# The output projection of a selective scan's reversed parts: from one block of work at steps 48 to 52 to two halves at steps 35 and 48

## The chip, the cores and the metric

The kernel runs on one core of a Trainium2 chip. The metric is device time of the whole launch in microseconds (us). The program is one launch of a four-layer network; the change touches only its first layer.

## The reference, cut to what matters

Layer 0 is a bidirectional selective scan (Mamba) on 2 images of 48 x 48 = 2304 tokens, 256 channels, 512 inner channels, 16 states. Layers 1 to 3 (linear attention, softmax attention, a graph mixture, sigmoid attention, a mixture of experts) follow and are not touched.

```python
def step(h, xs):                       # d_inner = 512, n = 16 states
    d_t, B_t, C_t, u_t = xs
    dA = jnp.exp(d_t[..., None] * A)
    h = dA * h + (d_t * u_t)[..., None] * B_t[:, None, :]
    y = jnp.einsum('bdn,bn->bd', h, C_t)
    return (h, y)
# a branch: xs = silu(causal depthwise conv(xi)); proj = xs @ xproj_w.T
#           dt = softplus(proj[:16] @ dtproj_w.T + b); B, C = rest of proj
#           y = (scan + xs * D) * silu(z)
# layer: xi, z = in_proj(norm(x)); forward branch + branch over the reversed tokens;
#        out = x + out_proj(y_forward + y_reversed)
```

## The kernel before, in words

`mamba_chunks` cuts each image into 5 parts of 461 tokens (`MT`; the last 460). A part takes 64 steps (`STEPS`), one for each of 16 states x 4 blocks of 128 inner channels. The 20 parts are numbered g = 0 to 19: 0 to 4 forward over image 0, 5 to 9 reversed over image 0, 10 to 14 and 15 to 19 the same for image 1. h is the next part, g + 1. Steps are counted S = 64 g + s.

At each step ScalarE (ACT) writes the exponential `DA(S)` into a PSUM bank (L778), GpSimd (POOL) multiplies `DBU` (L919), VectorE (DVE) runs the scan over the tokens (L963) and multiplies by C (`mix`, L974), and TensorE (PE) adds the product to y in PSUM with an identity matrix (L607, two passes in float32). DVE works in pairs of steps: two scans, mix, a small copy of the carried states, mix. ACT runs ahead of DVE by at most two scans, since there are two banks for `DA`; POOL by four; DVE may be ahead of PE by four products (`G` has four buffers).

Everything else is laid between the steps, at fixed step numbers written out by hand in each engine's loop: an engine works its own list in order, so what it waits for holds up the step's instruction behind it. While part g is scanned, the engines prepare part h: convolution (PE s = 11, 13, 16, 19; ACT takes it at 16 to 28: `take_conv`, `exp_conv`, `log_conv`, `sig_conv`), `xproj` (PE 36, ACT `take_pj` 44), `dt(h, 0)` (PE 42, ACT `dt_part` 47 to 52, `floor_rest` 56, POOL's sums at 52 to 63), and `dt(g, 1)` at 5. The gate z of a reversed part h is projected on PE at 55, 56, 59, 61 (`z`, L550) and taken by ACT at 58 to 63 (`take_z` L730, `exp_z` L735). `xi` (L492) projects the input of forward part g + 2. `first` (L590, L592) opens the four y banks 0 to 3 with D * xs and the stored forward y; `gate_y` (L951, DVE) multiplies the finished y of a reversed part by silu(z): blocks 0 and 1 at s = 34 of the part, 2 and 3 at s = 2 of the next.

The output projection of a reversed part is done during the part behind it: `out(g - 1, m, half)` on PE at s = 48, 49, 51, 52, m being the block of 128 output channels. It adds x (loaded into `XR`) with the identity (L564, 2 passes) and 4 products with `w_out` (L566, 8 passes) into PSUM bank m. ACT copies both banks into X at once at s = 55 (`take_out`, L754). This is so in parts 6 to 10 and 16 to 19; the last, part 19, is projected after the loop.

PSUM banks 0 to 3 hold y of the running part. Blocks 0 and 1 are finished with step 31, and from `gate_y` (or, in a forward part, `take_y` at ACT's step 35) until the next part begins banks 0 and 1 are free for xproj (bank 0), dt (0 and 1), the output projection, z and xi (0 and 1 in turn). Semaphores with the names `dt_base`, `o_ready`, `o_added`, `z_exp`, `y_taken` guard these uses.

The lines before the change that matter most:

```python
if is_rev(g - 1):
    if s == 48:
        out(g - 1, 0, 0)
    elif s == 49:
        out(g - 1, 0, 1)
    elif s == 51:
        out(g - 1, 1, 0)
    elif s == 52:
        out(g - 1, 1, 1)
...
if s == 55 and is_rev(g - 1):
    take_out(g - 1)
```

Of the kernel before, what the change touches and what calls it, by code (L numbers as in the profile page):

```python
# [313 lines left out]
def mamba_chunks(nc, ctx, k, A, w):  # L314
# [62 lines left out]
    with nc.Block() as block:  # L377
        @block.sync
        def _(sp):
# [43 lines left out]
            for g in range(NCH):  # L423
# [7 lines left out]
                if is_rev(g - 1):  # L431
                    b, at, n = tokens(g - 1)
                    if rev_before(g - 1):
                        sp.wait_ge(o_added, rev_before(g - 1))
                    sp.dma_start(XR[:, :, :n], A["x"][b].rearrange("(k p) n -> p k n", p=P)[:, :, at:at + n])\
                      .then_inc(xr_in, 16)
# [37 lines left out]
            sp.wait_ge(o_added, rev_before(NCH - 1))  # L474
            sp.dma_start(XR[:, :, :n], A["x"][b].rearrange("(k p) n -> p k n", p=P)[:, :, at:at + n]).then_inc(xr_in, 16)
            sp.wait_ge(o_added, rev_before(NCH))

        @block.tensor
        def _(pe):
            def xi(h, j):  # L480
                b, at, n = tokens(h)
                if j < 2 and h:
                    pe.wait_ge(dt_base, 2 * (h - 1) + 1)
                    if h >= 2 and rev_before(h - 2):
                        pe.wait_ge(o_added, rev_before(h - 2))
                    if is_rev(h - 1):
                        pe.wait_ge(z_exp, JD * rev_before(h))
# [40 lines left out]
            def dt(h, p):  # L528
                rev = chunk(h)[1]
                pe.wait_ge(pj_done, h + 1)  # L530
                if p:
# [9 lines left out]
            def z(h, j):  # L541
                b, at, n = tokens(h)
                if j < 2:
                    pe.wait_ge(dt_base, 2 * h + 1)
                    if rev_before(h - 1):
                        pe.wait_ge(o_added, rev_before(h - 1))
# [7 lines left out]
            def out(g, m, half):  # L554
                if half == 0:
                    pe.wait_ge(y_taken, 2 * g + 2)
                    if g + 2 < NCH:
                        pe.wait_ge(dt_base, 2 * (g + 2) + 1)
                    elif g + 1 < NCH:
                        pe.wait_ge(y_taken, 2 * (g + 1) + 1)  # L560
                    if rev_before(g):
                        pe.wait_ge(o_added, rev_before(g))
                    pe.wait_ge(xr_in, 16 * (rev_before(g) + 1))
                    pe.matmul(PS[:, m, :wide(g)], k.ident[:], XR[:, m, :wide(g)], start=True, stop=False)  # L564
                for j in range(2 * half, 2 * half + 2):
                    mm = pe.matmul(PS[:, m, :wide(g)], w.w_out[:, j, m * P:(m + 1) * P], Z[:, g % 2, j, :wide(g)],  # L566
                                   start=False, stop=(j == JD - 1))
                if m == 1 and half == 1:
                    mm.then_inc(o_ready, 1)

            def first(g, p):
                rev = chunk(g)[1]
                pe.wait_ge(xs_done, JD * (g + 1))
                if p == 0:
                    pe.wait_ge(dt_base, 2 * g + 1)
                    if g and rev_before(g - 1):
                        pe.wait_ge(o_added, rev_before(g - 1))
# [25 lines left out]
            for S in range(STEPS * NCH):  # L603
# [7 lines left out]
                if h < NCH:  # L611
# [10 lines left out]
                    elif s == 42:  # L622
                        dt(h, 0)
                if is_rev(g - 1):
                    if s == 48:
                        out(g - 1, 0, 0)
                    elif s == 49:
                        out(g - 1, 0, 1)
                    elif s == 51:
                        out(g - 1, 1, 0)  # L630
                    elif s == 52:
# [3 lines left out]
                if is_rev(h):  # L635
                    if s == 55:
                        z(h, 0)
                    elif s == 56:
                        z(h, 1)
                    elif s == 59:  # L640
                        z(h, 2)
                    elif s == 61:
# [12 lines left out]
        def _(act):  # L655
# [68 lines left out]
            def take_z(h, j):  # L724
# [3 lines left out]
                if j == 0 and taken:  # L728
                    act.wait_ge(o_ready, taken)
# [21 lines left out]
            def take_out(g):  # L751
                b, at, n = tokens(g)
                act.wait_ge(o_ready, rev_before(g) + 1)
                act.activation(k.X[:, :, b * L + at:b * L + at + n], PS[:, 0:KC, :n], ACT.Copy).then_inc(o_added, 1)  # L754
# [16 lines left out]
            for S in range(STEPS * NCH):  # L771
# [13 lines left out]
                if h < NCH:  # L785
# [14 lines left out]
                    elif s == 24:  # L800
                        take_conv(h, 3)
                    elif s == 25:
                        exp_conv(h, 3)
                    elif s == 26:
                        sig_conv(h, 0)
                    elif s == 27:
                        log_conv(h, 1)
                    elif s == 28:
# [7 lines left out]
                if s == 55 and is_rev(g - 1):  # L816
                    take_out(g - 1)
                if s == 35 and is_fwd(g):
                    take_y(g, 0)
                if is_rev(h):  # L820
                    if s == 58:
                        take_z(h, 0)
                    elif s == 59:
                        exp_z(h, 0)
# [29 lines left out]
            take_out(NCH - 1)  # L854
# [2854 lines left out]
```

## Time and profile before

| | us |
|---|---|
| median of 3 runs | 5767.82 |
| the runs | 5745.86, 5767.82, 5774.27 |
| the profiled execution | 5744.21 |
| its span | 5742.4 |
| first scan step to last of layer 0 | 150.7 to 2343 |

The span is the time from the first to the last instruction; the profiled execution's own time is 1.8 us longer. TensorE's mean granted clock is 0.928 of full speed. Over the whole span PE is busy for 4796.9 us (84%), DVE 3422.7 (60%), ACT 2068.0 (36%), POOL 2320.9 (40%); these are averages over stages with different limits. In timelines a float32 matmul shows as two passes, and passes that follow one another overlap in the record.

### The profile page before, as it was taken

To read this page: it belongs to the slowest core of one execution; us is meant where nothing else is said; L and a number is where in the kernel's file an instruction comes from. 1 tells how busy PE (TensorE), PEld (TensorE's weight loads), DVE (VectorE), ACT (ScalarE), POOL (GpSimd) and SP (SyncE) were. 2 spreads that over 40 slices of the span, in tenths; PEclk is the share of its full clock that TensorE was granted. 3 is DMA by queue.
4 is the path that set the end of the run, shared out by engine and by line. 5 is a ranking of instruction groups with operands and counts; after the bars stand their busy time and mean duration, and the time that the engine had idled before them with its cause. 6 is when DMAs were issued, how large, how long until landed. Compare 5 with 4: busy or idle time off the path is not lost. (4 is left out here: it accounts for less than half of the span.)

```text
span 5742.4 us, 53254 instructions
## 1 busy us (share of the span) xinstructions
PE 4796.9 (84%) x14970; PEld 2664.1 (46%) x14971; DVE 3422.7 (60%) x4924; ACT 2068.0 (36%) x3366; POOL 2320.9 (40%) x2102
## 2 busy tenths in 40 slices
PE   5887888888778887799799997484999899996897
PEld 3333333333333333355455654362555555555675
DVE  2999999999999999587495345483222101003013
ACT  2655656655566665232322221001222222222123
POOL 3888888888888888211112001380000000003002
PEclk8999999999999999999899997586999999995999
DMA  2434334433434433100101001100001000000232
GB/s 94 141 113 151 122 123 133 130 103 117 146 126 131 132 109 106 49 30 15 56 12 37 1 1 42 25 5 19 17 17 58 2 0 2 0 11 34 73 96 77
DMA packets 218043, 380.52 MB, mean 66 GB/s; under 512 B 34395, under 2 KB 205324, under 8 KB 212964
## 3 DMA queue, kind: packets, MB, share of 16 engines
q1 hardware_dynamic: 203796, 364.33, 19.9%
q0 software_dynamic: 7552, 7.81, 0.8%
q10 hardware_dynamic: 6480, 5.90, 0.4%
q8 instruction: 88, 1.44, 0.1%
q14 instruction: 127, 1.04, 0.1%
HBM read 331.84 MB, written 48.71 MB: 66 GB/s over the span
## 5 line engine op out<-in xcount | busy, mean ns | idle before, releaser
L607 PE MATMUL PS<-G,ident 128*128 128x461 f32 (+1 forms) x2560 | 1167.0, 583 | 404.9 <-DVE G L974 403.1
L919 POOL TENSOR_TENSOR DBU<-DU,BB 128x461 f32<-128x461 f32 (+1 forms) x1280 | 1371.9, 1086 | 324.1 <-DVE PS L963 312.5
L963 DVE TENSOR_TENSOR_SCAN PS<-PS,HC,DBU 128x461 f32<-128x461 f32 (+1 forms) x1024 | 1152.4, 1168 | 45.5 <-ACT PS L778 44.4
L778 ACT ACTIVATE PS<-DT,alog 128x461 f32<-128x461 f32 (+1 forms) x1280 | 824.8, 645 | 703.7 <-DVE PS L963 702.0
L607 PEld LDWEIGHTS PS<-G,ident 128*128 128x128 f32 x2560 | 462.3, 194 | 1075.2 <-DVE G L974 838.1
L974 DVE TENSOR_TENSOR G<-PS,CB 128x461 f32<-128x461 f32 (+1 forms) x1280 | 786.6, 625 | 11.1 <-PE PS L607 11.1
L2931 POOL TENSOR_TENSOR xs<-X 128x384 f32 x12 | 11.7, 990 | 829.6 <-issue 528.0
L2900 DVE TENSOR_TENSOR X<-X,PS 128x768 f32 x12 | 11.4, 954 | 554.9 <-PE PS L2867 554.9
L2795 DVE TENSOR_TENSOR Hg<-Hg,GB 128x384 f32<-128x384 f32 x192 | 106.8, 558 | 373.1 <-ACT Hg L2782 373.1
L2856 PE MATMUL PS<-QT,N 128*128 x864 | 312.0, 489 | 4.7 <-ACTq L2873 4.7
L963 DVE TENSOR_TENSOR_SCAN PS<-PS,DBU 128x461 f32<-128x461 f32 (+1 forms) x256 | 272.8, 1108 | 65.2 <-ACT PS L778 65.0
L2867 PE MATMUL PS<-AT,XT 128*128 128x384 f32 x864 | 310.5, 487 | 0.0
L1352 POOL TENSOR_TENSOR X<-X,FF x12 | 34.4, 2870 | 633.3 <-ACT EV L1347 633.3
L1028 PE MATMUL PS<-TT,w_fc 128*128 x768 | 278.5, 491 | 12.2 <-ACTq L1052 12.2
L2746 PE MATMUL PS<-NN,w1g 128*128 x768 | 278.0, 490 | 4.5 <-ACTq L2768 4.5
L2762 PE MATMUL PS<-Hg,w2g 128*128 128x384 f32 x768 | 276.4, 488 | 0.0
L1038 PE MATMUL PS<-H,w_fc 128*128 128x384 f32 x768 | 275.5, 486 | 0.0
L514 PE MATMUL PS<-XI,cdiag 128*128 128x461 f32 (+1 forms) x640 | 260.0, 549 | 0.6 <-ACT XI L663 0.6
L2889 ACT ACTIVATE AT<-PS 128x384 f32<-128x384 f32 x216 | 105.4, 490 | 417.8 <-PE PS L2856 417.7
L2782 ACT ACTIVATE Hg<-PS,b1g 128x384 f32<-128x384 f32 x192 | 110.8, 580 | 371.0 <-PE PS L2746 370.9
L1066 ACT ACTIVATE H<-PS,b_fc 128x384 f32<-128x384 f32 x192 | 110.7, 580 | 323.4 <-PE PS L1028 323.4
L2856 PEld LDWEIGHTS PS<-QT,N 128*128 128x128 f32 x864 | 164.9, 191 | 120.0 <-issue 6.9
(434 smaller groups left out, 7347.0 us busy)
## 6 DMA issues: line engine op xcount, KB each, us to landing
BB<-proj_dram SPq DMA_DIRECT2D x256, 461.0 KB, 3.8
CB<-proj_dram SPq DMA_DIRECT2D x64, 922.0 KB, 6.1
BB<-proj_dram SPq DMA_DIRECT2D x64, 460.0 KB, 4.6
ew<-in_l_w SPq DMA_DIRECT2D x16, 1024.0 KB, 6.9
CB<-proj_dram SPq DMA_DIRECT2D x16, 920.0 KB, 5.9
GB<-gate_dram SPq DMA_DIRECT2D x12, 768.0 KB, 4.1
w_fc<-in_l_w_fc SPq DMA_DIRECT2D x4, 2048.0 KB, 12.0
XI<-xi_dram SPq DMA_DIRECT2D x8, 928.0 KB, 5.1
```

The costliest lines, as they stand in the source:

```text
L514: mm = pe.matmul(PS[:, 2 + j % 2, :wide(h)], w.cdiag[:, j, t, :], XI[:, j, at:at + wide(h)], start=(t == 0), stop=(t == TAP - 1))
L607: pe.matmul(PS[:, j, :wide(g)], k.ident[:], G[:, S % 4, :wide(g)], start=False, stop=(n == DS - 1))\
L778: act.activation(DA(S), DT[:, j, :wide(g)], ACT.Exp, scale=w.alog[:, chunk(g)[1], j, n:n + 1]).then_inc(da_done, 1)
L919: pool.tensor_tensor(DBU[:, S % 4, :wide(g)], DU[:, j, :wide(g)], BB[:, 2 * u + n % 2, :wide(g)], ALU.mult).then_inc(dbu_done, 1)
L963: dve.tensor_tensor_scan(flow(HS(S), g), flow(DA(S), g), flow(DBU[:, S % 4, :wide(g)], g), start, ALU.mult, ALU.add).then_inc(h_done, 1)
L974: dve.tensor_tensor(G[:, S % 4, :wide(g)], HS(S), CB[:, n, :wide(g)], ALU.mult).then_inc(g_done, 1)
L1028: mm = pe.matmul(k.PS[:, s % 3, :T], w1(j, s), src(j, c), start=(j == 0), stop=(j == KC - 1))
L1038: mm = pe.matmul(k.PS[:, 4 + 2 * u + o, :T], w2(m, o), H[:, m, :], start=(m == 0), stop=(m == NM - 1))
L2746: mm = pe.matmul(k.PS[:, s % 3, :T], w1[:, j, s * P:(s + 1) * P], g.NN[:, j, bass.ds(c * T, T)], start=(j == 0), stop=(j == KC - 1))
L2762: mm = pe.matmul(k.PS[:, 4 + 2 * u + o, :T], w2[:, m, o * P:(o + 1) * P], H[:, m, :], start=False, stop=(m == NM - 1))
L2856: mm = pe.matmul(k.PS[:, s % NA, :T], k.N[:, j, s * P:(s + 1) * P], QT[:, j, bass.ds(c * T, T)], start=(j == 0), stop=(j == KC - 1))
L2867: mm = pe.matmul(k.PS[:, 4 + 2 * u + o, :T], XT[:, m, o * P:(o + 1) * P], AT[:, m % NA, :], start=(m == 0), stop=(m == LT - 1))
```

## The change

The output projection's two blocks m = 0 and m = 1 now both go through PSUM bank 1 (in the last part, behind the loop, still through bank m), one after the other. Block 0 is projected at steps 35 and 37, block 1 at steps 48 and 50. ACT copies each block by itself: at step 45 and at step 54. `o_ready` and `o_added` count blocks, so all their thresholds are multiplied by KC = 2. `dt(h, 0)` moves from step 42 to 43 in all parts and, behind a reversed part, waits for the first copy. z moves from 55, 56, 59, 61 to 52, 55, 58, 60, and its first piece, in bank 0, no longer waits for the output; ACT's first `take_z` moves from 58 to 57 and its `exp_z` to 58. On ACT `sig_conv(h, 0)` comes at 24, ahead of the last block's take and exponential, which go to 26 and 27, and the second `log_conv` and `sig_conv` to 28 and 29.

```diff
--- before.py
+++ after.py
@@ -431,7 +431,7 @@
                 if is_rev(g - 1):
                     b, at, n = tokens(g - 1)
                     if rev_before(g - 1):
-                        sp.wait_ge(o_added, rev_before(g - 1))
+                        sp.wait_ge(o_added, KC * rev_before(g - 1))
                     sp.dma_start(XR[:, :, :n], A["x"][b].rearrange("(k p) n -> p k n", p=P)[:, :, at:at + n])\
                       .then_inc(xr_in, 16)
                 for m in range(1, 5):
@@ -471,9 +471,9 @@
                 if g == LATE:
                     store_xi(g + 2)
             b, at, n = tokens(NCH - 1)
-            sp.wait_ge(o_added, rev_before(NCH - 1))
+            sp.wait_ge(o_added, KC * rev_before(NCH - 1))
             sp.dma_start(XR[:, :, :n], A["x"][b].rearrange("(k p) n -> p k n", p=P)[:, :, at:at + n]).then_inc(xr_in, 16)
-            sp.wait_ge(o_added, rev_before(NCH))
+            sp.wait_ge(o_added, KC * rev_before(NCH))
 
         @block.tensor
         def _(pe):
@@ -482,7 +482,7 @@
                 if j < 2 and h:
                     pe.wait_ge(dt_base, 2 * (h - 1) + 1)
                     if h >= 2 and rev_before(h - 2):
-                        pe.wait_ge(o_added, rev_before(h - 2))
+                        pe.wait_ge(o_added, KC * rev_before(h - 2))
                     if is_rev(h - 1):
                         pe.wait_ge(z_exp, JD * rev_before(h))
                 if j >= 2:
@@ -528,6 +528,8 @@
             def dt(h, p):
                 rev = chunk(h)[1]
                 pe.wait_ge(pj_done, h + 1)
+                if p == 0 and is_rev(h - 2):
+                    pe.wait_ge(o_added, KC * rev_before(h - 2) + 1)
                 if p:
                     if h:
                         pe.wait_ge(y_taken, 2 * h)
@@ -542,8 +544,8 @@
                 b, at, n = tokens(h)
                 if j < 2:
                     pe.wait_ge(dt_base, 2 * h + 1)
-                    if rev_before(h - 1):
-                        pe.wait_ge(o_added, rev_before(h - 1))
+                    if j and rev_before(h - 1):
+                        pe.wait_ge(o_added, KC * rev_before(h - 1))
                 else:
                     pe.wait_ge(z_exp, JD * rev_before(h) + j - 1)
                 for i in range(KC):
@@ -552,20 +554,24 @@
                 mm.then_inc(z_ready, 1)
 
             def out(g, m, half):
+                bank = 1 if g + 1 < NCH else m
                 if half == 0:
-                    pe.wait_ge(y_taken, 2 * g + 2)
-                    if g + 2 < NCH:
-                        pe.wait_ge(dt_base, 2 * (g + 2) + 1)
+                    if m == 0:
+                        pe.wait_ge(y_taken, 2 * g + 2)
+                        pe.wait_ge(xr_in, 16 * (rev_before(g) + 1))
+                        if g + 1 < NCH:
+                            pe.wait_ge(y_taken, 2 * (g + 1) + 1)
+                        if rev_before(g):
+                            pe.wait_ge(o_added, KC * rev_before(g))
                     elif g + 1 < NCH:
-                        pe.wait_ge(y_taken, 2 * (g + 1) + 1)
-                    if rev_before(g):
-                        pe.wait_ge(o_added, rev_before(g))
-                    pe.wait_ge(xr_in, 16 * (rev_before(g) + 1))
-                    pe.matmul(PS[:, m, :wide(g)], k.ident[:], XR[:, m, :wide(g)], start=True, stop=False)
+                        pe.wait_ge(o_added, KC * rev_before(g) + 1)
+                        if g + 2 < NCH:
+                            pe.wait_ge(dt_base, 2 * (g + 2) + 1)
+                    pe.matmul(PS[:, bank, :wide(g)], k.ident[:], XR[:, m, :wide(g)], start=True, stop=False)
                 for j in range(2 * half, 2 * half + 2):
-                    mm = pe.matmul(PS[:, m, :wide(g)], w.w_out[:, j, m * P:(m + 1) * P], Z[:, g % 2, j, :wide(g)],
+                    mm = pe.matmul(PS[:, bank, :wide(g)], w.w_out[:, j, m * P:(m + 1) * P], Z[:, g % 2, j, :wide(g)],
                                    start=False, stop=(j == JD - 1))
-                if m == 1 and half == 1:
+                if half == 1:
                     mm.then_inc(o_ready, 1)
 
             def first(g, p):
@@ -574,7 +580,7 @@
                 if p == 0:
                     pe.wait_ge(dt_base, 2 * g + 1)
                     if g and rev_before(g - 1):
-                        pe.wait_ge(o_added, rev_before(g - 1))
+                        pe.wait_ge(o_added, KC * rev_before(g - 1))
                     if rev:
                         pe.wait_ge(z_exp, JD * (rev_before(g) + 1))
                     if is_fwd(g + 1):
@@ -619,27 +625,27 @@
                         conv(h, 3)
                     elif s == 36:
                         xproj(h)
-                    elif s == 42:
+                    elif s == 43:
                         dt(h, 0)
                 if is_rev(g - 1):
-                    if s == 48:
+                    if s == 35:
                         out(g - 1, 0, 0)
-                    elif s == 49:
+                    elif s == 37:
                         out(g - 1, 0, 1)
-                    elif s == 51:
+                    elif s == 48:
                         out(g - 1, 1, 0)
-                    elif s == 52:
+                    elif s == 50:
                         out(g - 1, 1, 1)
                 if s == 31:
                     first(g, 1)
                 if is_rev(h):
-                    if s == 55:
+                    if s == 52:
                         z(h, 0)
-                    elif s == 56:
+                    elif s == 55:
                         z(h, 1)
-                    elif s == 59:
+                    elif s == 58:
                         z(h, 2)
-                    elif s == 61:
+                    elif s == 60:
                         z(h, 3)
                 if is_fwd(g + 2) and s in xi_at(g):
                     for j in range(JD):
@@ -726,7 +732,7 @@
                 act.wait_ge(z_ready, n + 1)
                 taken = rev_before(h) - is_rev(h - 1)
                 if j == 0 and taken:
-                    act.wait_ge(o_ready, taken)
+                    act.wait_ge(o_ready, KC * taken)
                 act.activation(Z[:, h % 2, j, :wide(h)], PS[:, j % 2, :wide(h)], ACT.Copy).then_inc(z_raw, 1)
 
             def exp_z(h, j):
@@ -748,10 +754,11 @@
                     act.wait_ge(yf_stored[p], 16 * fwd_before(g))
                 act.activation(YF[:, two(p), :wide(g)], PS[:, two(p), :wide(g)], ACT.Copy).then_inc(y_taken, 1)
 
-            def take_out(g):
+            def take_out(g, m):
                 b, at, n = tokens(g)
-                act.wait_ge(o_ready, rev_before(g) + 1)
-                act.activation(k.X[:, :, b * L + at:b * L + at + n], PS[:, 0:KC, :n], ACT.Copy).then_inc(o_added, 1)
+                bank = 1 if g + 1 < NCH else m
+                act.wait_ge(o_ready, KC * rev_before(g) + m + 1)
+                act.activation(k.X[:, m, b * L + at:b * L + at + n], PS[:, bank, :n], ACT.Copy).then_inc(o_added, 1)
 
             act.preload_act_table_set("natural_log_exp_and_others")
             for j in range(JD):
@@ -798,14 +805,14 @@
                     elif s == 23:
                         log_conv(h, 0)
                     elif s == 24:
+                        sig_conv(h, 0)
+                    elif s == 26:
                         take_conv(h, 3)
-                    elif s == 25:
+                    elif s == 27:
                         exp_conv(h, 3)
-                    elif s == 26:
-                        sig_conv(h, 0)
-                    elif s == 27:
+                    elif s == 28:
                         log_conv(h, 1)
-                    elif s == 28:
+                    elif s == 29:
                         sig_conv(h, 1)
                     elif s == 44:
                         take_pj(h)
@@ -813,15 +820,18 @@
                         dt_part(h, 0, s - 47)
                     elif s == 56:
                         floor_rest(h, 0)
-                if s == 55 and is_rev(g - 1):
-                    take_out(g - 1)
+                if s == 45 and is_rev(g - 1):
+                    take_out(g - 1, 0)
+                if s == 54 and is_rev(g - 1):
+                    take_out(g - 1, 1)
                 if s == 35 and is_fwd(g):
                     take_y(g, 0)
                 if is_rev(h):
-                    if s == 58:
+                    if s == 57:
                         take_z(h, 0)
+                    elif s == 58:
+                        exp_z(h, 0)
                     elif s == 59:
-                        exp_z(h, 0)
                         take_z(h, 1)
                     elif s == 60:
                         exp_z(h, 1)
@@ -851,7 +861,8 @@
                         take_xi(g + 1, 2)
                     elif s == 1:
                         take_xi(g + 1, 3)
-            take_out(NCH - 1)
+            for m in range(KC):
+                take_out(NCH - 1, m)
 
         @block.gpsimd
         def _(pool):
```

## Rows read from the trace of the kernel before

**Rows 1.** The page's costliest groups: busy, mean ns, idle before, releaser.
```profile
L963 DVE TENSOR_TENSOR_SCAN PS<-PS,HC,DBU 128x461 f32<-128x461 f32 (+1 forms) x1024 | 1152.4, 1168 | 45.5 <-ACT PS L778 44.4
```
**Rows 2.** Busy us by stretch (parts 1, 7): length, PE, PEld, DVE, ACT, POOL, clock.
```profile
253.60:359.50 105.90, 86.63 (x202) 36.46 (x200) 105.74 (x162) 64.61 (x97) 90.41 (x86) 0.97 0.41 126
...
898.90:1011.80 112.90, 95.18 (x230) 41.36 (x229) 108.26 (x163) 68.40 (x105) 94.00 (x89) 0.98 0.39 122
```
**Rows 3.** Timeline of DVE, steps 54 to 56: start us, us, engine, line; part 7, then part 10.
```profile
990.66 2.25 DVE L963 TENSOR_TENSOR_SCAN PS<-PS,HC,DBU 128x461 f32<-128x461 f32 x2
...
997.02 1.19 DVE L963 TENSOR_TENSOR_SCAN PS<-PS,HC,DBU 128x461 f32<-128x461 f32 x1 [2.98 <-ACT PS L778]
...
1340.14 1.13 DVE L963 TENSOR_TENSOR_SCAN PS<-PS,DBU 128x461 f32<-128x461 f32 x1 [3.34 <-ACT PS L778]
```
**Rows 4.** Timeline of ACT, steps 55 and 56 of part 7.
```profile
989.64 0.65 ACT L778 ACTIVATE PS<-DT,alog 128x461 f32<-128x461 f32 x1 [0.41 <-DVE PS L963]
995.51 0.94 ACT L754 ACTIVATE X<-PS 128x922 f32<-128x922 f32 x1 [5.22 <-PE PS L566]
...
996.91 0.96 ACT L722 ACTIVATE V<-V 128x922 f32<-128x922 f32 x1
```
**Rows 5.** Timeline of PE, steps 48 and 49 of part 7.
```profile
983.59 1.04 PE L607 MATMUL PS<-G,ident 128*128 128x461 f32 x2 [1.35 <-DVE G L974]
984.47 0.94 PE L564 MATMUL PS<-XR,ident 128*128 128x461 f32 x2
...
987.57 1.71 PE L566 MATMUL PS<-Z,w_out 128*128 128x461 f32 x4
```
**Rows 6.** Timeline of POOL, step 58 of part 7.
```profile
997.95 1.16 POOL L890 TENSOR_TENSOR DT<-DT,V 128x461 f32<-128x461 f32 x1 [4.01 <-ACT V L722]
```
**Rows 7.** Timelines of DVE, ACT and PE, steps 59 to 62 of part 7.
```profile
1008.04 2.25 DVE L963 TENSOR_TENSOR_SCAN PS<-PS,HC,DBU 128x461 f32<-128x461 f32 x2 [0.68 <-ACT PS L778]
...
1006.92 0.55 ACT L730 ACTIVATE Z<-PS 128x461 f32<-128x461 f32 x1 [1.97 <-PE PS L550]
...
1005.17 1.71 PE L550 MATMUL PS<-X,w_in 128*128 128x461 f32 x4
```
**Rows 8.** Timelines of DVE and ACT, steps 24 and 25 of part 7.
```profile
939.90 2.51 DVE L963 TENSOR_TENSOR_SCAN PS<-PS,HC,DBU 128x461 f32<-128x461 f32 x2
...
940.01 0.65 ACT L667 ACTIVATE XS<-PS,vec 128x461 f32<-128x461 f32 x1 [1.55 <-PE PS L514]
```
**Rows 9.** Timeline of PE, steps 32 to 42 of part 7.
```profile
963.81 1.04 PE L607 MATMUL PS<-G,ident 128*128 128x461 f32 x2 [2.51 <-DVE G L974]
964.78 3.30 PE L524 MATMUL PS<-XS,w_x 128*49 128x461 f32 x8
968.01 4.21 PE L607 MATMUL PS<-G,ident 128*128 128x461 f32 x10
973.70 1.04 PE L607 MATMUL PS<-G,ident 128*128 128x461 f32 x2 [1.48 <-DVE G L974]
```
**Rows 10.** Timelines of PE and ACT, steps 42 to 47 of part 7.
```profile
974.67 1.81 PE L537 MATMUL PS<-PJ,w_dt 17*128 17x461 f32 x4
...
975.38 0.65 ACT L778 ACTIVATE PS<-DT,alog 128x461 f32<-128x461 f32 x1 [1.56 <-DVE PS L963]
...
977.03 0.92 ACT L700 ACTIVATE E<-PS 128x922 f32<-128x922 f32 x1
```
**Rows 11.** Timelines of PE and DVE in part 6, and its stretch by clock.
```profile
849.82 1.42 PE L607 MATMUL PS<-G,ident 128*128 128x461 f32 x2 [2.51 <-DVE G L974]
851.17 4.57 PE L524 MATMUL PS<-XS,w_x 128*49 128x461 f32 x8
...
856.82 0.64 DVE L974 TENSOR_TENSOR G<-PS,CB 128x461 f32<-128x461 f32 x1 [0.99 <-PE PS L607]
...
850.40:853.80 3.40, 3.40 (x6) 0.86 (x5) 3.40 (x6) 1.30 (x2) 2.12 (x2) 0.50 0.00 0
```
**Rows 12.** Groups of ACT by line, layer 0: one bank copied.
```profile
L730 ACT ACTIVATE Z<-PS 128x461 f32<-128x461 f32 (+1 forms) x40 | 22.2, 555 | 53.1 <-PE PS L550 53.1
```

## The prediction

> **What bounds the kernel now.** I read the views in this order: the page's groups, the busy times by stretch, the timeline of VectorE (DVE) through one part, and at each of its gaps the timelines of the engine that it waited for.
>
> The page's dearest DVE group is the scan, which sat idle only 45.5 us before 1024 of its instructions, almost all of it for ScalarE's (ACT) exponentials [rows 1]. So in the scan stage DVE sets the pace, and only what makes DVE wait costs time. The stretches say how much: part 1 (forward, no output projection) takes 105.9 us with 105.74 busy; part 7 (reversed, behind a reversed part) takes 112.9 with 108.26 busy [rows 2]. 2.2 us of the difference is the two gatings of y; the other 4.6 are idle. By rows 2 a pair of steps is 105.9 / 32 = 3.31 us.
>
> Where the idle time lies: before the scan of step 56 DVE waits 2.98 us for ACT (3.34 in part 10) [rows 3], and I count 0.24 more before the scan of step 57 (0.30 in part 10). ACT had itself stood 5.22 us in front of L754, the copy of the finished output projection, which sits at its step 55; the exponential of step 56 is queued behind it [rows 4]. TensorE (PE) had no time to finish sooner: from step 48 it puts 20 passes of output projection between its accumulations without a pause (6 passes, then 4, per output block; the starts 984.47 and 987.57 enclose 8 passes, so 0.39 us each) [rows 5]. It is a stall by place and not by volume: nine parts have it (6 to 10, 16 to 19).
>
> **The change part by part.**
>
> *A. Stall at steps 56 and 57.* Half of the output projection goes to steps 35 and 37; only 10 passes stay, at steps 48 and 50. In the times of part 7: accumulation 48 starts at 983.59, block 1 begins at 984.47 as now, its second piece would be issued behind accumulations 49 and 50, and so is the last 4 of 14 passes in a row (6 + 2 + 2 + 4): the last one starts 13 x 0.39 after 984.47 and takes 0.55, end 990.1. ACT, which has its take at step 54, waits until then; the copy of one bank occupies 0.45 of ACT's issue time, so the exponential of step 55 starts at 990.55 instead of 989.64 [rows 4] and lets the scan start at 991.2. That scan isn't due before 990.66 + 1.1 = 991.76 [rows 3]. So the new wait has a margin of 0.5 us (0.2 in part 10, whose steps are shorter) and the old one is gone. What is late next: ACT's floor (L722) at step 56 now ends at about 993.4 instead of 997.8, and GpSimd's (POOL) subtraction, which sat 4.01 us idle for it [rows 6], follows its third product at 993.9 without a wait. POOL then has six products and four sums of 1.1 to 1.2 us to lay before step 63; I get each product 2 to 3 us ahead of its scan. Gain: 8 x 2.98 + 3.34 for step 56, 7 x 0.24 + 0.30 for step 57 (none in part 19): 27.2 + 2.0 = 29.2 us. Bounds: 0 if another thing releases ACT as late as now, 29.2 if nothing takes its place; I take 29.2 because the margins are positive at each step.
>
> *B. Gate projection z.* The four pieces move from steps 55, 56, 59, 61 to 52, 55, 58, 60. The first two lie beside work that has room now (the freed 10 passes, 3.9 us). The third matters: its copy held ACT until 1006.92, the exponential of step 62 came after it and DVE stood 0.68 [rows 7]. In rows 7 the z passes start at 1005.17, right behind two accumulations; one step earlier means two passes (0.78 us) earlier, so the exponential is done 0.78 sooner, 0.1 before the scan wants it. Ten parts have this stall (4 to 8, 14 to 18): 6.8 us. The fourth piece keeps its distance to the end of the part, so the 0.35 us at step 0 stays. Parts 9 and 10 have the same stall from the xi projection, which isn't moved, and so has the late xi at the end of part 8 (4.7 us at DVE): no gain there.
>
> *C. Order of the convolution's takes.* At step 24 ACT stood 1.55 us for the last convolution block; that made the scan of step 25 late by 0.15 (the pair's scans take 2.51 instead of 2.25, overlap apart) [rows 8]. A logistic that waits for nothing takes that place and the take goes to step 26. 19 parts, 15 x 0.15 + 4 x 0.33 = 3.6 us. It puts the last logistic one step later, still two steps before POOL's gating of its half. From both sides: nothing or 3.6.
>
> *D. The new pieces at steps 35 and 37.* PE is idle 2.51 us before accumulation 36, since DVE gates y there [rows 9]. Block 0's 6 passes (2.3 us) fit into that hole: it must wait for that gating to have left bank 1, which ends 0.1 us before accumulation 35 does. Its x rows were loaded at the start of the part. The other 4 passes (1.55 us) follow accumulation 37. In part 7 that accumulation ends at 968.8, the projection x_proj (8 passes, 3.30 us) before it [rows 9]. Then 38 to 41 end at 973.4, before accumulation 42 can start at 973.70: the slack that is there (1.48 us idle and the catching up) just takes it, and DVE's products of steps 40, 42, 44 find their buffers free. In part 10, forward and without the gating hole, accumulation 37 comes 0.8 us later and the product of step 40 about 0.4 us late: -0.4. ACT's take of block 0 at step 45 (0.56 us) stands in the 1.56 us idle before the next exponential [rows 10].
>
> The hole has a second side. In part 6 the same x_proj takes 4.57 us instead of 3.30 and DVE waits 0.99 at step 40; the granted clock of that stretch is 0.50, that is 1.2 instead of 2.4 GHz, and it fell behind the 2.51 us in which PE did nothing [rows 11]. Five of the nine parts have this (6, 9, 16, 18 with 0.98 to 0.99, part 17 with 2.43): 6.4 us. In parts 7 and 8 the clock stays up and the wait isn't there. With the hole filled I take all nine to go like part 7: 6.4 us. Other end: 0, the clock falls all the same.
> The Trainium skill ("TensorE: Matmul & The Clock Gate", section "HAM oscillation") says that a wait between bursts of matmuls lets the gate fall and that the next burst starts at half rate; rows 11 agree. But its Part 1 also says that the place of such transitions differs from run to run, by which this gain could be 0; the sum would then be 39.6 instead of 46.
>
> *E. dt projection one step later (43), with a wait for the take of block 0.* It ends at about 976.9 instead of 976.2; its reader on ACT starts at 977.03 [rows 10]. The take is issued before it on ACT (done at 974.5) and dt can't start before 975.3, so the wait is free. Queued behind dt on PE are accumulations 44 on, which DVE needs only at step 48. Where the clock is at its lower level there (the forward parts), dt ends some 1.3 us later; ACT then catches up by step 53, out of the 1.1 us that it idles there. Cost 0, at most 0.5 a part in all 19, 9 us.
>
> *F. Waits and counts.* All o_added and o_ready thresholds are rescaled. On the sync engine's queue the wait ahead of the load of x is met earlier than now. Ten more ACT instructions: 2 x 0.56 [rows 12] against 0.94 [rows 4], 0.2 us each in ACT's idle time. At the very end only the second block's copy follows the last matmul: 0.94 - 0.56 = 0.4 us gained.
>
> Sum: 29.2 + 6.8 + 3.6 + 6.4 - 0.4 + 0.4 = 46 us. All later stages are untouched. The profiled execution took 5744.2 us (5742.4 span, 1.8 around it), so one like it should take 5698. The runs shown are 5745.9, 5767.8 and 5774.3: with the profiled one they lie in two groups 25 us apart, which the scan stage doesn't explain. Their middle, over all four, is 5756.8, and less 46 that is **5711**; from the median 5767.8 it would be 5722, which is the same forecast in the upper group.
>
> **Rivals.**
> *R1, PE becomes late at steps 35 to 42.* For: five parts run that stretch at the lower clock now, and 10 passes more cost 3.9 us there, 7.7 at that clock. Against: the fill keeps PE working before it, and the extra pieces stand behind accumulations that DVE needs first. If the clock falls all the same and the second piece isn't caught up, D's 6.4 is lost and each of nine parts loses a further 1.55: 46 - 6.4 - 14 = 26 us, 5731.
> *R2, ACT's new take at step 54 waits too long.* For: margin only 0.5 us. If PE comes 2 us later than I worked out, DVE loses 1.5 in each of nine parts, 13.5: gain 32, 5725. Half of this case's times lie past the 0.5% bound.
> *R3, slower than before.* PE at its lower clock over steps 48 to 50. The accumulation, 6 passes, two accumulations and 4 passes then take 12.4 us instead of 6.2, the block ends at 996.3 and the scan of step 55 waits 5.6 in nine parts: 50 us lost, against 40 won: 10 us slower, 5767. It decides once the delay passes 5 us a part. Against: in none of the 19 parts does the clock fall between steps 46 and 57.
> *R4, nothing won:* the stall at 56 returns through another queue (POOL's late sums, which stand behind the same floor); 0 to 10 us won, 5750.
>
> **Numbers.** Forecast 0.66, R1 0.15, R2 0.11, R3 0.04, R4 0.04. A measurement tells 0.5%, here 29 us, from no change. Faster by over 0.5%: the forecast, half of R2 and a little of R1, 0.73; within: 0.22; slower: 0.05. Own range of the forecast: gains of 38 to 48 in either group of runs, 5696 to 5730. Reaching into R1 and R2 it becomes 5690 to 5745.
>
> **What would show it.** A: L754's successor waits about 1 us before step 55 and the scan of step 56 has no idle time; part 7 lasts about 109 us. B: no idle time at step 62 in parts 4 to 8, 0.68 left in 9 and 10. C: none at step 25. D: PE busy where the 2.51 us were, no half clock at x_proj in parts 6 to 9, no DVE wait at step 40 except a little in part 10. The forecast is wrong if DVE's idle time in parts 6 to 10 stays above 3 us each, or if it turns up at steps 40 to 44 or 55.

## The result, and the profile after

The changed kernel takes 5710.8 us (median of 5 runs, 5700.3 to 5723.4), the kernel before 5756.6 (5 runs); the ratio is 0.9917, 95% interval 0.9891 to 0.9943: 0.8% faster. A second set of runs of the changed kernel gave 0.9918 (0.9898 to 0.9937).

The two profiled executions differ by less, 5742.4 and 5721.6 us of span. So the scan stage is taken by itself from here on: from the start of the first scan to the start of the last it takes 2188.6 us before and 2139.8 after, 48.8 less. 28 us of that are hidden in this pair, 27 of them by a later stage that the change doesn't touch (last section).

Three parts (2, 8, 10) of the changed kernel by busy time. Columns: stretch, its length, busy us of PE, PEld, DVE, ACT, POOL with their instructions, granted clock, share and GB/s of DMA.

```profile
core 0: us, PE busy (x) PEld busy (x) DVE busy (x) ACT busy (x) POOL busy (x), PEclk, DMA share, GB/s
360.70:466.30 105.60, 83.69 (x201) 35.12 (x200) 105.60 (x161) 64.67 (x97) 89.47 (x85) 1.00 0.40 126
1001.80:1114.70 112.90, 99.23 (x241) 43.62 (x240) 107.91 (x163) 69.67 (x108) 94.70 (x90) 0.98 0.42 132
1225.80:1332.00 106.20, 90.06 (x222) 39.22 (x220) 103.26 (x163) 64.57 (x98) 89.59 (x85) 1.00 0.39 126
```

Part 2 now has no idle time of DVE, where part 1 had 0.2 [rows 2]. Part 8 is 112.9 us long but 4.8 of that is the late xi at its end, which it had before. Part 7, for which about 109 us were forecast, takes 110.1; 1.7 of that is a lower clock at its start, which comes up in two experiments below.

The page's group of the scan, to be read against [rows 1]: the idle time in front of it that ACT ended is 14.0 us for these 1024 instructions, after 44.4.

```profile
L974 DVE TENSOR_TENSOR_SCAN PS<-PS,HC,DBU 128x461 f32<-128x461 f32 (+1 forms) x1024 | 1150.0, 1167 | 14.0 <-ACT PS L785 14.0
```

Timelines of part 8 around steps 50 to 57, DVE, then ACT, then PE: these answer to [rows 3 to 5].

```profile
1093.33 2.25 DVE L974 TENSOR_TENSOR_SCAN PS<-PS,HC,DBU 128x461 f32<-128x461 f32 x2
...
1096.63 2.25 DVE L974 TENSOR_TENSOR_SCAN PS<-PS,HC,DBU 128x461 f32<-128x461 f32 x2
```
```profile
1091.25 0.65 ACT L785 ACTIVATE PS<-DT,alog 128x461 f32<-128x461 f32 x1 [1.13 <-DVE PS L974]
1092.77 0.56 ACT L761 ACTIVATE X<-PS 128x461 f32<-128x461 f32 x1 [0.87 <-PE PS L572]
1093.22 0.64 ACT L785 ACTIVATE PS<-DT,alog 128x461 f32<-128x461 f32 x1
1094.55 0.65 ACT L785 ACTIVATE PS<-DT,alog 128x461 f32<-128x461 f32 x1 [0.68 <-DVE PS L974]
1095.13 0.96 ACT L728 ACTIVATE V<-V 128x922 f32<-128x922 f32 x1
```
```profile
1087.15 0.94 PE L570 MATMUL PS<-XR,ident 128*128 128x461 f32 x2
1087.92 1.71 PE L572 MATMUL PS<-Z,w_out 128*128 128x461 f32 x4
1089.47 1.71 PE L613 MATMUL PS<-G,ident 128*128 128x461 f32 x4
1091.02 1.71 PE L572 MATMUL PS<-Z,w_out 128*128 128x461 f32 x4
```

Scans 54 and 56 start 3.30 us apart, and DVE has no idle time between them. ACT's wait for the output projection is 0.87 us instead of 5.22, and the exponential behind it ends at 1093.86, 0.56 before the scan of step 55 would start (1094.42). On PE block 1 takes 14 passes in a row, as worked out.

PE at steps 35 to 42, against [rows 9]:

```profile
1060.30 3.67 PE L613 MATMUL PS<-G,ident 128*128 128x461 f32 x8
1063.99 1.01 PE L570 MATMUL PS<-XR,ident 128*128 128x461 f32 x2
1064.84 1.71 PE L572 MATMUL PS<-Z,w_out 128*128 128x461 f32 x4
1066.48 1.04 PE L613 MATMUL PS<-G,ident 128*128 128x461 f32 x2
1067.45 3.30 PE L524 MATMUL PS<-XS,w_x 128*49 128x461 f32 x8
1070.68 1.04 PE L613 MATMUL PS<-G,ident 128*128 128x461 f32 x2
1071.56 1.71 PE L572 MATMUL PS<-Z,w_out 128*128 128x461 f32 x4
```

The 2.51 us hole is gone; x_proj takes 3.30 us in each of the eight changed parts that have one (part 19 prepares none).

The pairs of scans behind the two other edits, step 24 of part 2 (against [rows 8]) and step 62 of part 8 (against [rows 7]), start without a wait:

```profile
400.35 2.24 DVE L974 TENSOR_TENSOR_SCAN PS<-PS,HC,DBU 128x461 f32<-128x461 f32 x2
```
```profile
1106.53 2.25 DVE L974 TENSOR_TENSOR_SCAN PS<-PS,HC,DBU 128x461 f32<-128x461 f32 x2
```

To see where the 48.8 us lie I took the distance from each pair of steps to the next in both traces and summed the differences by place:

| place | edit | forecast | measured |
|---|---|---|---|
| steps 54 to 58, nine parts | A | -29.2 | -30.9 |
| steps 60 to 62, ten parts | B | -6.8 | -7.8 |
| step 24, 19 parts | C | -3.6 | -5.8 |
| steps 38 to 42 | D | -6.0 | -7.9 |
| steps 8 to 22 | none | 0 | +3.8 |
| the rest | E | 0 | -0.2 |

### The profile page after: what moved, and what is told of

It reads as the page before. It is cut to its first block and busy times, and to the rows that moved or that the text cites. A ratio compares the mean times of both kernels' runs of the same rounds, so it can differ in the third digit from the quotient of the medians.

```text
span 5721.6 us, 53254 instructions
## 1 busy us (share of the span) xinstructions
PE 4778.9 (84%) x14970; PEld 2657.9 (46%) x14971; DVE 3414.6 (60%) x4924; ACT 2073.3 (36%) x3376; POOL 2318.3 (41%) x2102
## 5 line engine op out<-in xcount | busy, mean ns | idle before, releaser
L613 PE MATMUL PS<-G,ident 128*128 128x461 f32 (+1 forms) x2560 | 1148.0, 575 | 384.9 <-DVE G L985 383.2
```

Source lines behind the costliest of these rows:

```text
L613: pe.matmul(PS[:, j, :wide(g)], k.ident[:], G[:, S % 4, :wide(g)], start=False, stop=(n == DS - 1))\
```

## The experiments

All numbers are of the scan stage (2188.6 us before, 2139.8 after), each from one profiled execution. The changed kernel's stage came out within 0.6 us when it was run again; how much the lower clock costs in it moves by more than that from kernel to kernel, so each result is also given by place, as in the table above. The times of the whole launch spread by more than most of these effects and don't tell the single edits apart.

**One edit alone: C.** On the kernel before, `sig_conv(h, 0)` to step 24, the last `take_conv`, `exp_conv` to 26 and 27, the second `log_conv`, `sig_conv` to 28 and 29.

> The kernel before with edit C alone (order of the convolution's logistic and take on ACT). Measured is the scan stage, from the start of the first scan to the start of the last: 2188.6 us before, 2139.8 after. Theory (each edit is worth the idle time of DVE that it takes away, and no more): no idle time at step 25, 3.6 us less, 2185.0; every other gap stays (2.98 at step 56, 0.68 at 62, 0.99 at 40). Rival (the take's place doesn't matter, ACT is late anyhow): the 0.15 us turn up at step 27 or 29, 2188.6.

Measured 2179.5, 9.1 less. No gap is left at step 25. By place: 5.8 at step 24, and 3.3 at steps 8 to 22 and 38 to 42, where the lower clock happened to cost less. So C is worth 5.8, more than the 3.6 which the printed idle times add up to. The reason is in the pair distance: steps 24 to 26 take 0.27 us less in each part though 0.15 was printed. Two scans in a row overlap by 0.1 us in the records ([rows 3]: x2 takes 2.25 with each 1.18); a scan that waits loses that too, so each of DVE's waits costs about 0.1 us more than its bracket says.

**One edit alone: B.**
```diff
-                    elif s == 59:
+                    elif s == 58:
                         z(h, 2)
-                    elif s == 61:
+                    elif s == 60:
                         z(h, 3)
```


> The kernel before with the third and fourth piece of z at steps 58 and 60 instead of 59 and 61, and nothing else. Theory: the 0.68 us before step 62 go in ten parts (4 to 8, 14 to 18), the gap at 56 stays, scan stage 2188.6 - 6.8 = 2181.8 us. Rival (B works only because A freed 10 passes): gone in parts 4, 5, 14, 15, which have no output projection, 2.7 us less, 2185.9.

Measured 2178.4. 7.8 at steps 60 to 62, all ten parts, with A's stall in place: B doesn't need the freed passes, and the rival falls. The other 2.4 us are the lower clock again: it left step 40 (-5.1) and came to steps 8 to 22 (+2.7).

**D's mechanism alone: the hole filled with useless work.**
```diff
+                if is_rev(g) and s == 35:
+                    pe.wait_ge(y_taken, 2 * g + 1)
+                    for j in range(3):
+                        pe.matmul(PS[:, 1, :wide(g)], w.ddiag[:, 1, j, :], XS[:, g % 2, j, :wide(g)], ...)
```


> The kernel before with three useless matmuls (6 passes) put on PE at step 35 of each reversed part, into the free bank 1, where PE is idle for 2.51 us. The result isn't used. Theory of D (the idle hole is what lets the clock fall, and the slow x_proj behind it makes DVE wait at step 40): no lower clock at steps 37 and 38, no wait at step 40 in parts 6, 9, 16, 17, 18, nor in 5 and 15; 6.4 + 2.5 = 8.9 us less, 2179.7. The gap at 56 stays at 2.98. Rival (the clock falls with the low load of x_proj itself, or by chance): same places at the lower clock, 2188.6 or a little more.

Measured 2182.0. DVE waits at step 40 in none of the parts, the lower clock is nowhere at steps 37 and 38, and the sum there is -9.65 us over all seven that had it. More work on PE made the scan stage 6.6 us shorter, where 8.9 were expected: 3.0 us came back at steps 8 to 22, mostly in parts 7 and 16, behind the other hole (below), which the expectation left out. The whole launch, run once, took 5754.0 us and shows no gain. Part 6, to be read against [rows 11]:

```profile
844.13 2.57 PE L636 MATMUL PS<-XS,ddiag 128*128 128x461 f32 x6
846.80 1.04 PE L607 MATMUL PS<-G,ident 128*128 128x461 f32 x2
847.77 3.30 PE L524 MATMUL PS<-XS,w_x 128*49 128x461 f32 x8
```

That this isn't the chance of one execution shows when all 13 traces (both kernels and the eleven experiments) are counted, over the nine reversed parts that have an x_proj: with the hole open the clock fell at steps 36 to 39 in 37 of 57 parts, with the hole filled, by useless or by moved work, in 0 of 60.

**What is left without moving the work: two takes only.** All 20 passes at steps 48 to 52 in banks 0 and 1, takes at 54 and 57, all else as before.

> The changed kernel with all 20 passes of the output projection back at steps 48, 49, 51, 52 in banks 0 and 1, z, dt and the convolution's order as before; what is left of the change is that ACT takes each block by itself, at steps 54 and 57. Theory (the 10 passes moved to step 35 are what counts; PE has 20 + 16 passes and 14 accumulations between steps 48 and 61, 24.8 us of work for 23.2 of time): the gap at 56 goes, but the first take of z, queued behind, waits for PE, and DVE waits about 2 us before step 59; scan stage 2188.6 - 9 x 1.1 = 2179 us. Rival (two takes by themselves are enough, the stall was only one of ACT's order): 2188.6 - 29 = 2160 us.

Measured 2176.1; at steps 54 to 58 the nine parts win 12.0 us of the 30.9. Part 7, ACT and then DVE:

```profile
995.77 0.55 ACT L757 ACTIVATE X<-PS 128x461 f32<-128x461 f32 x1 [1.56 <-PE PS L568]
...
999.64 0.56 ACT L732 ACTIVATE Z<-PS 128x461 f32<-128x461 f32 x1 [2.78 <-PE PS L550]
```
```profile
1000.77 1.19 DVE L969 TENSOR_TENSOR_SCAN PS<-PS,HC,DBU 128x461 f32<-128x461 f32 x1 [1.81 <-ACT PS L781]
```

The wait moved to the next thing that PE owes ACT, the first piece of z (in parts 9 and 10 of xi), and DVE loses 2.0 us there in each of eight parts. So 12 us of A come from emptying the blocks one by one. The other 19 come with the rest: 10 passes out of PE's crowded stretch, and z's first pieces earlier. In parts 9 and 10, whose xi stands at the same steps in both kernels, the changed kernel hasn't this wait either, so there the moved passes do it. The move with a single take wasn't run, so the split of 12 and 19 holds for this order only. The prediction called the stall one of place, not of volume: half of that is wrong, the stretch from step 48 to 61 was overfull.

**dt one step later, alone** (`s == 42` to `s == 43` for `dt(h, 0)`).

> The kernel before with the dt projection at step 43 instead of 42 in all parts, and nothing else. In the changed kernel the lower clock at step 45 is gone from all parts that had it. Theory: dt's place does that: accumulation 43 now lies ahead of dt, none of the parts 1 to 4 and 11 to 14 shows the lower clock at step 45, and the time is the same, since nothing waited there: scan stage 2188.6 (within 1). Rival (the shift of all later work against the clock's own grid did it): the lower clock at 45 stays in the forward parts.

Measured 2187.3, 1.3 less where at most 1 was expected, and nothing of the difference lies at dt's own steps: it is the lower clock at step 40 (-2.7) and at steps 8 to 22 (+1.6). The lower clock at step 45 is gone in all forward parts. PE in part 4 of this kernel, and the clock of that stretch, which was 0.50 for 6.8 us before:

```profile
645.43 1.81 PE L607 MATMUL PS<-G,ident 128*128 128x460 f32 x4 [1.48 <-DVE G L974]
647.17 1.80 PE L537 MATMUL PS<-PJ,w_dt 17*128 17x460 f32 x4
```
```profile
644.00:653.00 9.00, 6.28 (x15) 2.61 (x16) 9.00 (x15) 6.39 (x10) 6.15 (x6) 1.00 0.60 165
```

Four accumulation passes follow the 1.48 us gap, where two did, and the 17-row dt comes after. The fall at step 45 is itself a matter of chance: in the five kernels with dt at step 42 it came in 8, 2, 1, 4 and 4 of the eight forward parts 1 to 4 and 11 to 14. In the eight with dt at 43 it came in 0 of 64, so dt's place is shown to matter by all of them together. That PE ran slower there cost DVE nothing, so this is worth no time.

**The margin of A.** The changed kernel with block 1 two steps later.
```diff
-                    elif s == 48:
+                    elif s == 50:
                         out(g - 1, 1, 0)
-                    elif s == 50:
+                    elif s == 52:
                         out(g - 1, 1, 1)
```


> The changed kernel with block 1 two steps later (50 and 52 instead of 48 and 50), its take still at step 54. The prediction gave that take a margin of 0.5 us. Theory: block 1 then ends at about 992.65 in the times of part 7 instead of 990.1, the scan of step 55 can start at 993.8 and was due at 991.8: DVE waits 2.0 us before step 55 in nine parts, scan stage 2139.8 + 18 = 2158. Rival (ACT has more room than was worked out): under 0.5 us a part, below 2144.

Measured 2166.5, 26.6 more than the changed kernel where 18 were expected: 27.1 more at steps 54 to 58, 1.6 of that a wait at step 59 of part 10, and 0.5 less elsewhere. Part 7, ACT and DVE:

```profile
986.96 0.56 ACT L761 ACTIVATE X<-PS 128x461 f32<-128x461 f32 x1 [4.17 <-PE PS L572]
```
```profile
988.09 1.18 DVE L974 TENSOR_TENSOR_SCAN PS<-PS,HC,DBU 128x461 f32<-128x461 f32 x1 [2.68 <-ACT PS L785]
```

The stall returns at step 55 and not at 56, in nine parts. It is 2.7 us instead of the 2.0 expected, because the expectation let block 1 start 0.8 us too early: accumulation 50 must wait for its product first. The step numbers matter this much: two steps are most of A's gain.

**The hole that A left: dt(g, 1) at step 3 instead of 5.** In part 7 of the changed kernel (PE, DVE, and the stretch by clock) the half clock begins behind the 2.51 us hole made by the other gating of y, and lasts 10.2 us:

```profile
902.47 2.46 PE L613 MATMUL PS<-G,ident 128*128 128x461 f32 x4 [2.51 <-DVE G L985]
904.86 3.44 PE L539 MATMUL PS<-PJ,w_dt 17*128 17x461 f32 x4
```
```profile
909.85 1.18 DVE L974 TENSOR_TENSOR_SCAN PS<-PS,HC,DBU 128x461 f32<-128x461 f32 x1 [0.22 <-ACT PS L785]
911.24 1.18 DVE L974 TENSOR_TENSOR_SCAN PS<-PS,HC,DBU 128x461 f32<-128x461 f32 x1 [0.21 <-ACT PS L785]
...
929.90 0.64 DVE L985 TENSOR_TENSOR G<-PS,CB 128x461 f32<-128x461 f32 x1 [0.99 <-PE PS L613]
```
```profile
903.50:913.70 10.20, 10.20 (x14) 3.72 (x13) 9.77 (x16) 6.66 (x10) 8.59 (x9) 0.50 0.15 46
```

> The changed kernel with the second dt projection at step 3 instead of 5. The changed kernel runs at the lower clock for 10.2 us from step 6 in parts 7, 17 and 19, behind the 2.5 us in which PE is idle while DVE gates y at step 2, and DVE waits there before steps 10, 11 and at 20 (1.4, 1.4, 0.8 us). Theory (an unfilled hole): dt's 4 passes fill it, no lower clock at steps 5 to 12, 3.7 us less, 2136.1. Rival (the clock falls by the light work of dt, wherever it stands): it falls at steps 3 to 8 still, 2139.8 or more.

Measured 2135.2, 4.6 less, 4.2 of it at steps 8 to 22; no wait of DVE is left at steps 10, 11 and 20 of the reversed parts behind another. The clock still falls at step 5 or 6 in some parts, but for 3.4 or 6.8 us, and dt stands ahead of it. So the first half of the theory fails: the lower clock did not end. One execution can't show that it got shorter, as its length changes by chance too; but the three kernels with dt at step 3 have no fall of 10.2 us and lose nothing behind it at steps 8 to 22, while eight of the ten with dt at step 5 have one to four such falls.

**The same cure for xi in parts 9 and 10.** PE 52, 55, 58, 60, takes 57, 59, 61, 63, no wait for the output ahead of the first piece.

> The changed kernel with the projection xi of parts 9 and 10 moved as z was: PE steps 52, 55, 58, 60 instead of 55, 56, 59, 60, takes at 57, 59, 61, 63 instead of 58, 59, 61, 62, and no wait for the output's takes ahead of the first piece. Theory: the same cure works for the same stall: 0.68 and 1.35 us go in part 9, 0.68 and 1.41 in part 10, 4.1 us less, 2135.7; the 4.7 + 1.1 at the end of part 8 stay. Rival: the last take only moves the wait to the first step of the next part, 1.4 us less, 2138.4.

Measured 2137.3: 4.5 less at steps 58 to 62 of the two parts, all their waits gone, and 2.2 more at steps 8 to 22, where the fall of 10.2 us came in four parts instead of three. The 4.7 and 1.1 behind part 8 stay.

**Both of these.**

> The changed kernel with both the second dt projection at step 3 and xi in parts 9 and 10 at 52, 55, 58, 60. By the single edits: 2139.8 - 4.4 (xi) - 4.2 (steps 8 to 22) = 2131.2 us. Rival (they share a cause, since each moves work around the lower clock): 2133 to 2136.

Measured 2130.8: -4.5 at steps 58 to 62 and -4.5 at steps 8 to 22. They add.

**The changed kernel again.**

> The changed kernel once more, word for word. The other runs showed the lower clock at other steps in each kernel, and the changed kernel lost 3.8 us at steps 8 to 22 of parts 7, 17 and 19 behind it. Theory: where the lower clock falls depends on how the execution happens to lie in time; all other gaps of DVE repeat to 0.1 us, the ones behind the lower clock move to other parts, scan stage 2137 to 2142 us. Rival (the pattern belongs to the kernel): the same parts 7, 17, 19, and 2139.8 within 0.3. The time of the whole: 0.9917 of before, the spread of some 25 us in it lies in the edge sums of the graph mixture (260 or 287 us) and not in the scan stage.

Measured 2140.4. Edits A, B and C repeat to 0.1 us. The falls of 10.2 us behind the hole at step 2 now come in parts 6 and 8, where DVE waits, and in none of 7, 17 and 19; and the clock falls at step 38 in both of parts 5 and 15: +1.45 us at steps 38 to 42, -0.8 at 8 to 22. So the place of the lower clock changes from execution to execution of the same kernel. In these two, a fall of 10.2 us cost 1.7 us in each of parts 6, 7, 8 and 17, and 1.05 in part 19, whose steps 16 to 22 carry no convolution.

**Two edits more.** To the kernel with both: the three useless matmuls at step 35 of parts 5 and 15 only, and
```diff
                     take_xi(g + 2, 0)
-                    take_xi(g + 2, 1)
-                if g == LATE + 1:
-                    if s == 0:
-                        take_xi(g + 1, 2)
-                    elif s == 1:
-                        take_xi(g + 1, 3)
+                if g == LATE + 1 and s < 3:
+                    take_xi(g + 1, s + 1)
```


> As the run before, and two edits more: in the two reversed parts without an output projection beside them (5 and 15) three useless matmuls fill PE's hole at step 35, and at the end of part 8 only the first take of xi stands ahead of the next part's first exponential, the others follow at its steps 0, 1 and 2. Theory: no lower clock at steps 37 and 38 of parts 5 and 15, 1.3 us less each time it fell there (1 to 2 of 2 parts); DVE's 4.7 + 1.1 us at the start of part 9 become 3.2 + 0.9 or so, 1.9 us less; scan stage 2127 to 2128 us, and the whole 0.989 to 0.990 of before. Rival: the later takes hold up the products of part 9's first steps (PE opens y behind them), nothing or less than nothing is won there, 2129 or more.

Measured 2128.0, 60.6 less than the kernel before; ratio of the whole 0.9906 (0.9881 to 0.9931). Against the changed kernel's 0.9918 on the same chip the intervals overlap, so that this one is faster rests on the scan stage alone: 12.4 us, 0.2%. The start of part 9:

```profile
1108.56 1.19 DVE L974 TENSOR_TENSOR_SCAN PS<-PS,HC,DBU 128x461 f32<-128x461 f32 x1 [3.20 <-ACT PS L789]
1110.43 1.19 DVE L974 TENSOR_TENSOR_SCAN PS<-PS,HC,DBU 128x461 f32<-128x461 f32 x1 [0.69 <-ACT PS L789]
```

3.2 + 0.7 instead of 4.7 + 1.1, and a new 0.45 before step 3: 1.4 won of the 1.9 expected. No lower clock in parts 5 and 15.

## Why the prediction was right, step by step

The forecast of 46 us was met in its mechanisms: 48.8 in the scan stage, 0.4 at the end. That is 49.2, a little over the prediction's own range of 38 to 48. That the medians differ by 45.8, and that 5711 was hit to 0.2 us, is luck: a stage that the change doesn't touch takes anything from 257 to 289 us (last section). The profiled execution, forecast at 5698, took 5723.4 for that reason. Luck is also in how the terms fell: edits A to D gave 6.8 us more than forecast together, and the unforeseen loss at steps 8 to 22 took 3.8 back.

*A* was right in mechanism and size (-30.9 for -29.2), and the margin that carried it was seen: the exponential is done 0.56 us ahead, worked out as 0.5. What the prediction didn't separate is that the split alone gives 12, and 19 need the moved passes. Its division of part 7's extra 7.0 us into 2.2 of gating and 4.6 idle leaves 0.2 unnamed, which moves no term.

*B* and *C* were right in place and 1.0 and 2.2 too small. The failing is the same: the prediction summed printed idle times, and each wait also costs the 0.1 us by which DVE's instructions otherwise overlap. With 46 waits removed that is nearly the whole difference of A, B and C to the forecast (44.5 against 39.6).

*D* was right: the hole filled, the clock stayed up around x_proj in all nine parts, and filling it with useless work alone ends the same waits. Part 10 lost 0.27 by the bracket and 0.38 by step distance, where 0.4 was forecast. -7.9 contains one wait of part 15 (1.4 us), a part that the edit doesn't touch, which went by the clock's chance; without it D is -6.5 for -6.0. The other end that the prediction gave for D, a gain of 0 since the clock falls elsewhere in each run, is answered by the counts above: its place does change, but behind a filled hole it fell in 0 of 60 parts.

*E* cost nothing, as said. The forecast overlooked the sister of D's hole: at step 2 of each part behind a reversed one DVE gates y as well, PE idles the same 2.51 us, and before the change the clock fell there for 3.4 us in three parts without hurting, and for 6.8 us in part 10, which lost 0.6. In the changed kernel it lasts 10.2 us in three parts and costs 4.4 there; with part 10's 0.6 gone, 3.8 in all. Why it lasts longer isn't settled; the same long fall came in runs with B, the filler or the dt step alone, and in none with C alone or before the change, so it doesn't belong to one edit.

*Rivals.* None came. R1 (PE late at steps 35 to 42) needed the clock to fall in spite of the fill, which it did in none of the parts with an output projection. R2 is refuted by the margin, and the run with block 1 two steps later shows how near it was. R3 needed the lower clock at steps 48 to 50 and R4 a wait for POOL; inside the changed kernel's scan stage the trace has neither.

## What to carry to other kernels

In a hand-staged loop, follow each gap of the engine that sets the pace back to the instruction that its releaser was stuck on; move the awaited work out of the crowded stretch and take it in pieces, and then check what the releaser is owed next. Count such a gap by the distance between steps with and without it and not by the printed idle time. Look for holes of TensorE just ahead of work that is due soon: that work may run at the lower clock (here x_proj took 4.57 us instead of 3.30), and a good filler is work taken from the crowded stretch.

## What the hardware showed that was not expected

Useless matmuls paid: 6 passes, 2.3 us of PE, in each reversed part, removed seven waits and 9.65 us at step 40 of the scan stage, because behind an idle 2.51 us TensorE's granted clock fell to 0.50 (1.2 GHz) while x_proj ran, and behind filled ones it didn't (37 of 57 open holes against 0 of 60 filled, over all traces).

Most of the spread of the whole kernel's time lies in one stage, the edge sums of the graph mixture: 257 to 289 us over 13 profiled executions, with the same instructions. What is left without this stage and the scan stage takes 3291 to 3304 us. The changed kernel's profiled execution, then the one with xi moved, over that stage:

```profile
3625.60:3912.60 287.00, 161.43 (x1030) 113.55 (x1030) 149.84 (x272) 1.84 (x8) 161.69 (x128) 0.72 0.08 6
```
```profile
3619.90:3879.90 260.00, 153.22 (x1030) 112.22 (x1030) 151.19 (x272) 1.83 (x8) 164.72 (x128) 0.78 0.08 7
```

No engine is busy for more than 165 us of it, and POOL and DVE do the same work in both in the same time, so most of the 27 us is waiting, with PE at its lower clock for a little longer (8 us more of PE's busy time). It came in groups (257 to 260 in six executions, 277 to 289 in the other seven), and what it waits for was not followed. It is of the size of the 25 us between the runs that the prediction could not explain, though runs without a profile don't show where they lost them, and more than half of what the change gives: the change could be read in the scan stage of one profile and needs many runs in the whole.
